# Narrow one-hots of an edge-counting step built by one comparison of two broadcast operands, with packed register words

## The chip, the core and the metric

The kernel runs on one core of a Trainium2 chip. The time is the device time of one execution in microseconds. The engines are named as in the profile: PE (TensorE matmul), PEld (its weight loads), DVE (VectorE), ACT (ScalarE), POOL (GpSimd) and SP (SyncE). A queue item is marked with q, as in DVEq: that is work of the engine's own sequencer (register arithmetic, loads of a register from memory, branches).

## The reference

A graph network on 3125 nodes and 103125 edges, sorted by destination, followed by an edge-conditioned attention layer.

```python
def _L0_gnn_ref(x, edge_index, W1, b1, W2, b2, W3, b3):
    ...
    deg = jax.ops.segment_sum(jnp.ones_like(col, dtype=x.dtype), col, num_segments=N)
    deg_inv_sqrt = jnp.where(deg > 0, jax.lax.rsqrt(jnp.maximum(deg, 1e-12)), 0.0)
    norm = deg_inv_sqrt[row] * deg_inv_sqrt[col]
    def gcn_layer(h, W, b):
        h = h @ W
        msg = norm[:, None] * h[row]
        agg = jax.ops.segment_sum(msg, col, num_segments=N)
        return agg + b
    h = jax.nn.relu(gcn_layer(x, W1, b1))
    h = jax.nn.relu(gcn_layer(h, W2, b2))
    return gcn_layer(h, W3, b3)
...
x = _layernorm(x + _L0_gnn_ref(...), axis=-1)
x = _layernorm(x + _L1_gnn_ref(x, edge_attr_16, ..., src, dst), axis=-1)
```

The first network's three gathers are computed as dense products with a matrix of counts: how many edges lead from each source to each destination. Building that matrix is the step that is changed.

## The kernel before

The counts are an SBUF table of 128 partitions by 25 blocks of destinations. They are filled window by window: a window is 20 destination nodes (WIN), there are 158 windows (NWIN), and a loop of 79 turns does two of them a turn, v = 0 and v = 1. The edges are sorted by destination, 128 to a tile, so a window needs few tiles of edges: six are always done (BASE), and a window that has more does the others one by one in an inner loop, the tail. For each tile DVE builds two one-hot matrices and PE multiplies them, adding the six or more products of a window in one PSUM bank:

- the wide one-hot, `hot_key`, 128 x 500, says for each edge which of 25 source blocks and 20 destinations it has (line 1130);
- the narrow one-hot, `hot_low`, 128 x 128, says which of 128 sources within the block (line 1132);
- PE loads the narrow one as weights and streams the wide one through (line 658). The two windows of a turn go to two banks, named `bank` and `pair` in the rows.

ACT copies each finished bank into the table (line 869). Between its copies ACT also does other work for the ordering of the nodes: 26 passes that count edges below a node (line 852), and 25 rankings (line 923), one in front of every second turn from turn 19 on.

The six tiles go in three groups of two (GROUP). DVE signals s_hot behind a group; PE signals s_hot_free behind its two matmuls. `hot` has four slots, so that two groups are in flight, and a fifth for tails:

```python
for a in range(BASE // GROUP):
    at = v * (BASE // GROUP) + a
    dve.wait_ge(s_hot_free, w * (2 * BASE // GROUP) + at + 1)
    for k in range(GROUP):
        hot_row = one_hot(at % 2 * GROUP + k, v, slice(a * GROUP + k, a * GROUP + k + 1))
    hot_row.then_inc(s_hot, 1)
    if a == 1:
        dve.wait_ge(s_hot, w * (2 * BASE // GROUP) + at)
        near(i * 2 + v + 1, 1 - v).then_inc(s_near, 1)
n = dve.value_load(win_count[0:1, bass.ds(i * 2 + v, 1)], min_val=1, max_val=DEPTH)
```

`near` (lines 1121 to 1126) fetches the next window's numbers: it loads a register with the window's first tile from `win_start`, shifts 16 columns of `edge_key` by the window's offset into `near_key`, and copies 16 columns of `edge_low` into `near_low`. The tile count of a window is loaded from `win_count` by DVE (line 1153) and by PE (line 670). PE ends each window with a drain that signals s_full to ACT (line 676). `plane_tables` (lines 1110 to 1118) fills `win_start` and `win_count` with six short instructions on one partition, once ahead of each of three layers.

When all windows are done, DVE waits for ACT's last copy, and the three gathers and the sorting of edges into units of eight follow; then the long loop of the attention layer, which is 1700 us of the span. None of their code is changed, except that the loops of nodes to themselves are added with another identity matrix (line 1176).

## Time and profile before

| | us |
|---|---|
| median of 3 runs | 2688.94 (2686.95 to 2690.07) |
| profiled execution | 2685.97 |
| its span, first to last instruction | 2684.2 |
| counting stage, about 42 to 664 us of the span | 622 |
| DVE busy in the counting stage | 496.35 |
| PE busy in the counting stage | 457.97 |

The span is divided into stages by what the lines do: preparation to 42 us, counting to 664 us, the gathers and the sorting of edges into units to about 930 us, the attention loop to about 2640 us, and the end. The difference of 1.8 us between the execution and its span lies around the program. The duration of an instruction in a row includes some tens of nanoseconds in which the next one already runs, so the cost of one in a dense sequence is the distance of two starts, not the duration.

### The profile page before, as it was taken

How to read it: one execution, taken by the hardware profiler on the slowest of the kernel's cores; microseconds unless marked ns; L12 is line 12 of the kernel's file. 1: busy time of each engine (PE TensorE's matmuls, PEld its weight loads, DVE VectorE, ACT ScalarE, POOL GpSimd, SP SyncE). 2: the span in 40 equal slices, each digit the busy share in tenths (PEclk: the TensorE clock that was granted, in tenths of full speed). 3: DMA queues.
4: the chain of work that ended last, by engine and by line, in shares of the span. 5: the costliest groups of instructions: out<-in, count | busy, mean ns of one | idle time of the engine just before them, and what ended most of it. 6: DMA issues, size and time to landing. Idle time of an engine off the chain costs nothing.

```text
span 2684.2 us, 39375 instructions
## 1 busy us (share of the span) xinstructions
PE 2030.2 (76%) x5872; PEld 714.5 (27%) x5873; DVE 2113.0 (79%) x4340; ACT 1413.4 (53%) x4967; POOL 1288.1 (48%) x1556
## 2 busy tenths in 40 slices
PE   3766777777699648887888888888888788888782
PEld 1111111111333313333333333333333333333330
DVE  5876888887401149999999999999999889999883
ACT  5123333321001047777767777777776666766762
POOL 2100000012455477666666666666666665666653
PEclk9655555555898859999999999999999999999996
DMA  2000000000000011110000000101000000100110
GB/s 32 14 0 26 0 0 0 0 0 1 20 11 11 16 13 11 10 10 10 10 9 10 10 10 9 10 10 10 9 10 10 10 9 10 9 10 10 10 7 9
DMA packets 87256, 26.29 MB, mean 10 GB/s; under 512 B 63117, under 2 KB 84223, under 8 KB 87103
## 3 DMA queue, kind: packets, MB, share of 16 engines
q0 software_dynamic: 37824, 18.62, 6.4%
q1 hardware_dynamic: 49327, 6.96, 1.7%
q10 hardware_dynamic: 80, 0.43, 0.1%
q8 instruction: 10, 0.16, 0.0%
q14 instruction: 15, 0.12, 0.0%
HBM read 23.30 MB, written 2.51 MB: 10 GB/s over the span
## 4 chain that ended last, share of the span: by engine, by line
issue 28%; DVE 26%; PE 17%; DVEq 15%; POOL 5%; POOLq 4%; ACT 3%; DMA 1%; ACTq 0%; PEldq 0%; SPq 0%; PEld 0%
PE pair L801 10%; DVE eo L1392 7%; DVEq L1409 3%; DVE top L1407 3%; ACT eo L988 3%; PE bank L658 3%; DVE hot L1132 3%; DVE hot L1130 3%; PE pair L658 2%; DVE top L1410 2%; DVE eo L1430 2%; DVEq L1417 2%; DVE rden L1445 2%; DVEq L1153 2%; PE pw L788 1%
## 5 line engine op out<-in xcount | busy, mean ns | idle before, releaser
L617 POOL DMA_INDIRECT nbr<-table,rec x960 | 963.7, 1004 | 463.1 <-issue 258.2
L801 PE MATMUL pair<-eo,ident 128*128 128x512 f32 x1856 | 903.0, 632 | 123.0 <-DVE eo L1430 120.1
L988 ACT ACTIVATE eo<-pw,nbr 128x32 f32<-128x32 f32 x3776 | 686.9, 407 | 0.0
L801 PEld LDWEIGHTS pair<-eo,ident 128*128 128x128 f32 x1856 | 364.8, 202 | 603.1 <-issue 586.9
L1392 DVE TENSOR_TENSOR eo<-pw,nbr 128x1024 f32 (+1 forms) x357 | 417.0, 1218 | 43.4 <-PE pw L788 42.9
L1130 DVE TENSOR_SCALAR hot<-iota_key,near_key 128x500 bf16<-128x500 f16 x974 | 341.0, 350 | 119.3 <-issue 55.5
L788 PE MATMUL pw<-wk,termsT 100*128 100x512 bf16 x954 | 288.5, 384 | 128.6 <-issue 64.6
L977 ACT ACTIVATE eo<-eo 128x2048 f32<-128x2048 f32 x117 | 223.5, 1910 | 206.1 <-DVE eo L1421 206.1
L658 PE MATMUL bank<-hot 128*128 128x500 bf16 x488 | 230.3, 603 | 127.2 <-DVE hot L1132 103.5
L1430 DVE TENSOR_TENSOR eo<-eo x232 | 273.5, 1221 | 30.9 <-issue 27.1
L658 PE MATMUL pair<-hot 128*128 128x500 bf16 x486 | 228.5, 602 | 51.6 <-DVE hot L1132 45.4
L1421 DVE TENSOR_TENSOR eo<-eo,bank (+1 forms) x117 | 266.4, 2277 | 0.0
L1132 DVE TENSOR_SCALAR hot<-iota_low,near_low 128x128 bf16<-128x128 bf16 x974 | 246.3, 253 | 0.0
L966 ACT CAST termsT<-pt 100x512 bf16<-100x512 f32 x240 | 139.3, 581 | 100.9 <-PE pt L770 100.9
L544 POOL TENSOR_SCALAR place<-place 128x25 f32<-128x25 f32 x1 | 0.3, 253 | 384.3 <-ACTq L927 384.3
L770 PE MATMUL pt<-identb,terms 128*100 128x128 bf16 x960 | 95.9, 223 | 116.0 <-ACT termsT L966 87.7
L611 POOL DMA_INDIRECT attr<-in_edge_attr_dram,rec x120 | 115.6, 964 | 136.5 <-DMA rec<-unit_recs 98.4
L869 ACT CAST counts<-pair 128x500 f32 x79 | 45.5, 576 | 225.2 <-PEq L676 225.2
L869 ACT CAST counts<-bank 128x500 f32 x79 | 45.5, 576 | 197.8 <-PEq L676 195.5
L788 PEld LDWEIGHTS pw<-wk,termsT 100*128 100x128 bf16 x954 | 68.1, 97 | 286.7 <-issue 286.4
L1407 DVE TENSOR_TENSOR top<-eo 128x1024 f32 (+1 forms) x117 | 142.7, 1220 | 0.0
L770 PEld LDWEIGHTS pt<-identb,terms 128*100 128x100 bf16 x960 | 78.0, 127 | 235.6 <-issue 235.6
(237 smaller groups left out, 1834.7 us busy)
## 6 DMA issues: line engine op xcount, KB each, us to landing
nbr<-table,rec POOLq DMA_INDIRECT x960, 2.4
rec<-unit_recs SPq DMA_DIRECT2D x122, 8.0 KB, 1.7
attr<-in_edge_attr_dram,rec POOLq DMA_INDIRECT x120, 2.5
unit_recs<-place SPq DMA_DIRECT2D x27, 64.0 KB, 1.6
shared<-key_row SPq DMA_DIRECT2D x1, 1600.0 KB, 6.7
counts<-in_dst_dram SPq DMA_DIRECT2D x1, 448.0 KB
counts<-in_src_dram SPq DMA_DIRECT2D x1, 448.0 KB
place<-in_src_dram,at_i POOLq DMA_INDIRECT x26, 2.6
```

The lines of the kernel that those rows point to most:

```text
L617: pool.indirect_dma_start(nbr[:, b, j * FEAT:(j + 1) * FEAT], None, table, bass.IndirectOffsetOnAxis(ap=rec[:, b, j:j + 1], axis=0)).then_ ...
L658: return pe.matmul(bank[v][:, 0:NG * WIN], hot_low[:, k, :], hot_key[:, k, :], start=first, stop=False, skip_group_check=True)
L788: mm = pe.matmul(pw[:, 2 * (k % 2) + j, :], termsT[:, unit, lo:lo + P], wk[:], start=True, stop=True)
L801: mm = pe.matmul(total, ident[:], eo[:, ring, j * 2 * CH:(j + 1) * 2 * CH], start=False, stop=(j == SLOT - 1), skip_group_check=True)
L977: act.activation(here, here, ACT.Exp).then_inc(s_ex, 1)
L988: done = act.activation(eo[:, ring, lo:lo + wide], pw[:, j - 4, c * wide:(c + 1) * wide], ACT.Copy, scale=nbr[:, held, j * FEAT + c:j * FE ...
L1130: dve.tensor_scalar(hot_key[:, slot, :].rearrange("p (a d) -> p a d", a=NG), iota_key[:], near_key[v][:, k], None, ALU.is_equal)
L1132: return dve.tensor_scalar(hot_low[:, slot, :], iota_low[:], near_low[v][:, k], None, ALU.is_equal)
L1392: dve.tensor_tensor(eo[:, bass.ds(ring, 1), k * 4 * CH:(k + 1) * 4 * CH] .rearrange("p r (c f) -> p (r c) f", f=2 * FEAT), pw[:, 2 * (k % ...
L1407: dve.tensor_tensor(wide(top4[:]), attention(ring, 0, 4), attention(ring, 4, 8), ALU.max).then_inc(s_attr_free, 1)
L1421: dve.tensor_tensor(here, here, wide(after).unsqueeze(1).broadcast_to([P, SLOT, FEAT, FEAT]), ALU.subtract).then_inc(s_d, 1)
L1430: dve.tensor_tensor(here, here, attention(ring, 4 * half, 4 * half + 4), ALU.mult).then_inc(s_p, 1)
```

## The change

The narrow one-hots of a window's six tiles are no longer six comparisons with a scalar per partition. One `tensor_tensor` of 128 x 768 compares the numbers 0 to 127, repeated for six tiles, with six columns of `edge_low`, each repeated 128 times. It stands in `near`, behind the shift of `edge_key`, and writes one of two buffers, `lows[v]`: one in `hot`, the other over `x1`, which is not in use yet. `near_low` and its copy go. `near` is called after the third group instead of the second. `hot` holds six slots instead of four, so that three groups can be in flight, and one for tails.

`win_start` and `win_count` become one table of words, two windows to a word. DVE and PE each load one word a turn (DVE after the first group of v = 1, for the turn behind it; PE after the first group of v = 0) and take first tile and count out of it by register arithmetic. `plane_tables` gets four more short instructions. `identh` goes, its use is taken by `identb`. The copies of `edge_key` and `edge_low` are narrower.

```diff
-        near_low = [sb(f"near_low{v}", [P, DEPTH], BF16, conv) for v in range(2)]
+        lows = [hot_low[:, 0:BASE, :], x1[:].rearrange("p t f -> p (t f)").bitcast(BF16)[:, 0:BASE * P].rearrange("p (k n) -> p k n", n=P)]
...
-                                mm = count(at % 2 * GROUP + k, a == 0 and k == 0)
+                                mm = count(a * GROUP + k, lows[v][:, a * GROUP + k, :], a == 0 and k == 0)
                             mm.then_inc(s_hot_free, 1)
-                        n = pe.value_load(win_count[0:1, bass.ds(i * 2 + v, 1)], min_val=1, max_val=DEPTH)
+                            if v == 0 and a == 0:
+                                pe.reg_mov(pe_word, pe.value_load(win_word[0:1, bass.ds(i, 1)], min_val=0,
+                                                                  max_val=(1 << 2 * WORD) - 1))
+                        pe.reg_alu(pe_n, pe_word, v * WORD, ALU.logical_shift_right)
+                        pe.reg_alu(pe_n, pe_n, DEPTH - 1, ALU.bitwise_and)
...
-            dve.sem_inc(s_hot_free, 2)
+            dve.sem_inc(s_hot_free, BASE // GROUP)
...
+                dve.scalar_tensor_tensor(out=win_row_g[:, 0, :], in0=win_row_g[:, 0, :], scalar=float(DEPTH),
+                                         in1=win_row_g[:, 1, :], op0=ALU.mult, op1=ALU.add)
...
-            def near(window, v):
-                t0 = dve.value_load(win_start[0:1, bass.ds(window, 1)], min_val=0, max_val=NB)
-                dve.tensor_scalar(near_key[v][:], edge_key[:, bass.ds(t0, DEPTH)], win_off[:, bass.ds(window, 1)],
-                                  None, ALU.add)
-                return dve.tensor_copy(near_low[v][:], edge_low[:, bass.ds(t0, DEPTH)])
+            def near(window, v, first):
+                to = dve.snap(first, min_val=0, max_val=NB)
+                key = dve.tensor_scalar(near_key[v][:], edge_key[:, bass.ds(to, DEPTH)], win_off[:, bass.ds(window, 1)],
+                                         None, ALU.add)
+                dve.tensor_tensor(lows[v],
+                                  iota_low[:].unsqueeze(1).broadcast_to([P, BASE, P]),
+                                  edge_low[:, bass.ds(to, BASE)].unsqueeze(2).broadcast_to([P, BASE, P]), ALU.is_equal)
+                return key
...
-                                hot_row = one_hot(at % 2 * GROUP + k, v, slice(a * GROUP + k, a * GROUP + k + 1))
+                                hot_row = hot_keys(a * GROUP + k, v, slice(a * GROUP + k, a * GROUP + k + 1))
                             hot_row.then_inc(s_hot, 1)
-                            if a == 1:
+                            if v == 1 and a == 0:
+                                dve.reg_mov(word_next, word_at(i + 1))
+                            if a == 2:
+                                first_of(1 - v, word if v == 0 else word_next)
                                 dve.wait_ge(s_hot, w * (2 * BASE // GROUP) + at)
-                                near(i * 2 + v + 1, 1 - v).then_inc(s_near, 1)
+                                near(i * 2 + v + 1, 1 - v, first).then_inc(s_near, 1)
```

`hot_keys` is the first half of the old `one_hot`. The tail keeps the comparison with one column for its narrow one-hot, now straight from `edge_low`.

On DVE, the last group of window v = 0 and what follows it up to the test for a tail stood like this before (ISA and REGISTER_ALU are the sequencer's own):

```order
L1145 REGISTER_ALU
L1130 TENSOR_SCALAR hot<-iota_key,near_key0 128x500 [waits s_hot_free]
L1132 TENSOR_SCALAR hot<-iota_low,near_low0 128x128
L1130 TENSOR_SCALAR hot<-iota_key,near_key0 128x500
L1132 TENSOR_SCALAR hot<-iota_low,near_low0 128x128
L1153 ISA
L1153 TENSOR_LOAD win_count
L1153 ISA x2
L1154 COMPARE_AND_BRANCH
```

The same place on DVE in the changed kernel, where line 1160 is the wide one-hot:

```order
L1160 TENSOR_SCALAR hot<-iota_key,near_key0 128x500 [waits s_hot_free]
L1160 TENSOR_SCALAR hot<-iota_key,near_key0 128x500
L1150 REGISTER_ALU
L1140 ISA [waits s_hot]
L1141 REGISTER_ALU
L1141 TENSOR_SCALAR near_key1<-edge_key,win_off 128x16
L1143 ISA
L1143 TENSOR_TENSOR x1<-iota_low,edge_low 128x768
L1185 REGISTER_ALU
L1186 REGISTER_ALU
L1187 ISA
L1188 COMPARE_AND_BRANCH
```

The fetch for the next window, with the wide comparison in it, now stands between the last group and the test for a tail; the register load in front of the test is gone.

On PE, the end of window v = 0 before:

```order
L658 MATMUL bank0<-hot 128x500 [waits s_hot]
L658 MATMUL bank0<-hot 128x500
L670 ISA
L670 TENSOR_LOAD win_count
L670 ISA x2
L671 COMPARE_AND_BRANCH
```

And the whole window on PE in the changed kernel:

```order
L660 MATMUL bank0<-hot 128x500 [waits s_hot]
L660 MATMUL bank0<-hot 128x500
L673 ISA
L673 TENSOR_LOAD win_word
L673 ISA x3
L660 MATMUL bank0<-hot 128x500 [waits s_hot]
L660 MATMUL bank0<-hot 128x500
L668 REGISTER_ALU
L660 MATMUL bank0<-hot 128x500 [waits s_hot]
L660 MATMUL bank0<-hot 128x500
L675 REGISTER_ALU
L676 REGISTER_ALU
```

PE's load has moved from behind the last matmul to behind the second one of v = 0, and window v = 1 has none.

## Rows read from the trace of the kernel before

**Rows 1.** Stretches: length, busy us of PE, PEld, DVE, ACT, POOL; then clock.
```profile
188.00:216.00 28.00, 5.72 (x12) 1.03 (x12) 6.89 (x33) 13.05 (x54) 2.74 (x12) 0.50 0.23 63
...
42.00:664.00 622.00, 457.97 (x973) 83.50 (x974) 496.35 (x2265) 182.77 (x271) 54.78 (x68) 0.55 0.03 6
467.00:477.00 10.00, 5.03 (x18) 1.02 (x18) 8.51 (x42) 4.78 (x5) 0.00 (x0) 1.00 0.00 0
```

**Rows 2.** Group by line, 42 to 664 us: busy us, mean ns, idle.
```profile
L1130 DVE TENSOR_SCALAR hot<-iota_key,near_key 128x500 bf16<-128x500 f16 x974 | 341.0, 350 | 119.3 <-issue 55.5 <-PE bank L658 36.3 <-PE pair L658 25.7
```

**Rows 3.** The timeline of DVE: start, duration, work, idle time before it.
```profile
360.89 0.35 DVE L1130 TENSOR_SCALAR hot<-iota_key,near_key 128x500 bf16<-128x500 f16 x1 [0.64 <-issue]
361.16 0.25 DVE L1132 TENSOR_SCALAR hot<-iota_low,near_low 128x128 bf16<-128x128 bf16 x1
361.32 0.35 DVE L1130 TENSOR_SCALAR hot<-iota_key,near_key 128x500 bf16<-128x500 f16 x1
...
362.75 0.23 DVE L1124 TENSOR_SCALAR near_key<-edge_key,win_off 128x16 f32 x1
362.89 0.17 DVE L1126 COPY near_low<-edge_low 128x16 bf16 x1
363.24 0.35 DVE L1130 TENSOR_SCALAR hot<-iota_key,near_key 128x500 bf16<-128x500 f16 x1 [0.18 <-PE bank L658]
...
364.34 0.35 DVE L1130 TENSOR_SCALAR hot<-iota_key,near_key 128x500 bf16<-128x500 f16 x1 [0.16 <-issue]
...
366.69 0.35 DVE L1130 TENSOR_SCALAR hot<-iota_key,near_key 128x500 bf16<-128x500 f16 x1 [0.22 <-PE pair L658]
...
368.27 0.35 DVE L1130 TENSOR_SCALAR hot<-iota_key,near_key 128x500 bf16<-128x500 f16 x1 [0.64 <-issue]
```

**Rows 4.** The timeline of PE in the same pair of windows.
```profile
362.19 1.84 PE L658 MATMUL bank<-hot 128*128 128x500 bf16 x4 [0.86 <-DVE hot L1132]
...
365.64 1.85 PE L658 MATMUL pair<-hot 128*128 128x500 bf16 x4 [0.39 <-DVE hot L1132]
367.69 1.01 PE L658 MATMUL pair<-hot 128*128 128x500 bf16 x2 [0.20 <-DVE hot L1132]
```

**Rows 5.** The timeline of PE where the clock rises, at 388 us.
```profile
384.37 1.84 PE L658 MATMUL bank<-hot 128*128 128x500 bf16 x4 [0.90 <-DVE hot L1132]
386.41 1.71 PE L658 MATMUL bank<-hot 128*128 128x500 bf16 x3 [0.20 <-DVE hot L1132]
388.52 1.02 PE L658 MATMUL pair<-hot 128*128 128x500 bf16 x4 [0.40 <-issue]
```

**Rows 6.** Queue instructions of the count load: duration in ns, least, median, most.
```profile
L1153 DVEq TENSOR_LOAD <-win_count x158: 299/304/317, 44.8 to 662.8; - x158
...
L1153 DVEq ALU_OP  x79: 40/40/40, 48.0 to 662.8; - x79
```

**Rows 7.** DVE groups by form, whole span.
```profile
L1392 DVE TENSOR_TENSOR eo<-pw,nbr 128x1024 f32 x348 | 406.2, 1218 | 23.2 <-PE pw L788 23.1
...
L1410 DVE TENSOR_TENSOR top<-top 128x512 f32<-128x512 f32 x117 | 81.0, 692 | 10.8
...
L1445 DVE RECIPROCAL rden<-pair 128x256 f32 x25 | 43.8, 1751 | 0.0
...
L1176 DVE TENSOR_TENSOR counts<-counts,identh 128x3072 f16<-128x3072 f16 x1 | 1.8, 1758 | 0.3 <-issue 0.3
```

**Rows 8.** The timeline of ACT around the ranking's start.
```profile
187.31 0.58 ACT L869 CAST counts<-pair 128x500 f32 x1 [2.87 <-PEq L676]
...
212.64 2.96 ACT L923 ACTIVATE gp<-shared,place 128x3200 int8<-128x3200 f32 x1 [14.57 <-DMA shared<-key_row]
```

**Rows 9.** The timeline of POOL behind the last rank, and its next work.
```profile
588.53 0.25 POOL L544 TENSOR_SCALAR place<-place 128x25 f32<-128x25 f32 x1 [384.31 <-ACTq L927]
...
621.42 0.95 POOL L549 DMA_INDIRECT place_records<-place  x1 [0.30 <-issue]
675.70 0.46 POOL L552 PARTITION_ALL_REDUCE deg_max<-deg_p  x1 [53.33 <-DVEq L1235]
```

More of the change, by code:

```diff
@@ L656, in count_plane, with count @@
                     for v in range(2):
-                        def count(k, first):
-                            return pe.matmul(bank[v][:, 0:NG * WIN], hot_low[:, k, :], hot_key[:, k, :],
+                        def count(k, low, first):
+                            return pe.matmul(bank[v][:, 0:NG * WIN], low, hot_key[:, k, :],
                                              start=first, stop=False, skip_group_check=True)
@@ L1103, in _ @@
             windows = dve.alloc_register("dve_windows")
+            word, word_next, first, tiles = (dve.alloc_register(f"dve_{v}") for v in ("word", "next", "first", "count"))
             mid = dve.alloc_register("dve_mid")
```

70 lines of the change are left out of this document (47 added, 23 removed).

## The prediction

> **What bounds the kernel now.** I read the table of stretches first. The counting stage takes 622 us, 23% of the span, and nowhere in it is an engine full: DVE is busy 496 us and PE 458 [rows 1]. So the order of events in one turn of the loop has to be read, in the timelines. DVE starts turns at 360.89 and 368.27, 7.38 us apart [rows 3]. 79 turns are 583 us. The rest of the stage is about 22 us in which the banks wait for ACT (below) and some 17 us for 26 tails: the wide one-hot ran 974 times, 158 x 6 and 26 more [rows 2], so a tail costs about 0.65 us.
>
> Within a turn DVE's sequence sets the pace. A wide one-hot holds DVE 0.27 us (360.89 to 361.16), a narrow one 0.16 (361.16 to 361.32): 12 x 0.43 = 5.1 us [rows 3]. The two fetches and four kinds of idle time make up the other 2.3. Two of these are the sequencer: from the first instruction of the last group to the next window 1.10 us pass at the window turn and 1.58 at the loop turn, though the group's own four instructions hold DVE only 0.85; the rows name "issue" as what ended these idle times, 0.16 and 0.64 [rows 3]. In that chain sits a register load of 0.30 us, where a step of register arithmetic takes 0.04 [rows 6]. At 363.24 and 366.69 DVE waits for PE to free a slot, 0.18 and 0.22 us [rows 3].
>
> PE follows closely, at the lower clock: the stage's mean is 0.55 [rows 1], and nearly all of it is spent at 1.2 GHz. Four matmuls take 1.84 us and two 1.01, so one adds 0.415 us [rows 4]. Between windows PE idles 0.39 and 0.86 us [rows 4]. The 0.39 isn't all waiting for DVE: behind a tail, with DVE ahead, it is 0.40 and ended by "issue" [rows 5]. It is PE's own price for the drain and the branch. The 0.86 has the loop's branch in it as well, and I take it whole.
>
> **DVE after the change.** Per window: six wide one-hots, 6 x 0.27 = 1.6 us; the shift of the keys, 0.14 (362.75 to 362.89) [rows 3]; and the one comparison of 128 x 768. That form isn't in the trace. The nearest rows are f32 tensor_tensors, one of which also reads an operand repeated along the innermost dimension (the 128 x 1024 one with nbr): 512 elements take 692 ns and 1024 take 1218 [rows 7], or 1.03 ns an element. For 768 that is 0.955 us, and since an instruction's duration overlaps the next one's by 0.08 (0.35 against 0.27 [rows 3]), it holds DVE 0.87 us. The sum is 2.61 a window, **5.2** a turn. The two copies of near_low, about 0.1 each, are gone.
>
> The other bound is a 2-byte tensor_tensor of 3072 elements in 1758 ns, 0.57 ns an element, where the repeated operand is a whole row [rows 7]. At that rate 768 elements take 0.55 us and hold DVE 0.47: 4.4 a turn. I take the slower rate, since it is the only one shown for a value repeated within a row. The Trainium skill has a rule for each: "VectorE: DVE Perf Modes", section "The perf-mode tier table", gives tensor_tensor on 2-byte data in SBUF two elements a cycle; "Vector Engine (DVE) Microarchitecture Reference", section 5.1, says that one element read 16 times as either source of such an operation ran at one a cycle. No row here shows the second; by it the turn is 5.2, by the first 4.4 before exposed sequencer time.
>
> The sequencer's chain: the load of 0.30 and the arithmetic on it leave the window turn; steps of 0.04 take their place, some 0.3 us for first tile, count and the two addresses. I estimate 1.0 us at the window turn and 1.45 at the loop turn, from the last group's start. DVE then has 2 x 0.27 + 0.14 + 0.87 = 1.55 us to do, so both are **hidden**. At 0.47 for the comparison it has 1.15, and 0.3 shows at the loop turn: 4.7. The one load a turn that DVE keeps stands behind the first group of v = 1, 0.5 us of work queued ahead of it and the rest of the comparison: nothing. The wait for s_hot in front of the fetch asks for the group before; its last instruction ends while the last group's two run. Behind it only the next window's groups are queued. The wait for a slot goes: three groups are in flight, and a slot is freed a whole window ahead.
>
> **PE after the change.** At 1.2 GHz, with DVE ahead, six matmuls in a row take 1.84 + 2 x 0.415 = 2.67 us. A turn is 2 x 2.67 + 0.39 + 0.86 = **6.6 us**, more than DVE's 5.2. At 2.4 GHz a matmul adds 0.21, six take about 1.02 + 2 x 0.21 = 1.44 [rows 5], and a turn needs 4.1: DVE bounds. PE's load now stands behind two matmuls, which cover it at 1.2 GHz and all but about 0.3 at 2.4, where PE has 1 us to spare. So everything hangs on the clock. What the rows show: the clock rose at 388 us right behind seven matmuls with one short gap, two windows joined by a tail [rows 5]; other rises in the stage look alike. It lasted from 3 to 10 us, as at 467 to 477, where PE was busy half the time at full clock [rows 1]. After the change PE at 1.2 GHz runs six matmuls without the gap of 0.20 in every window, which is closer to what went before the rises than today's four and two; so the half clock ends itself soon. At full clock PE is busier than in those ten microseconds, since the turn is 5.2 and not 7. I take a fifth of the turns at half clock: 0.8 x 5.2 + 0.2 x 6.6 = **5.5 us a turn**.
>
> **The rest.** Turns: 79 x (7.38 - 5.5) = 148.5 us gained. ACT's block of passes and the wait for the key row behind it, from 187.3 to the end of the first ranking at 215.6, doesn't shrink [rows 8]; PE can work one turn into it, now a shorter one: 2 lost. Tails are kept at 0.65, since their two instructions are the same and stand behind the comparison. plane_tables has four more instructions of 0.2 to 0.3 us in a dependent chain, in three layers: 3 to 4 lost, part of it beside the sorting on POOL. The first comparison has nothing in front: 0.7 lost. Narrower copies and identh: under 0.3 gained. Net 148.5 - 2 - 3.5 - 0.7 = **144 us**. What would be late next? ACT ranks 3.15 us at a time in front of two turns; a finished bank is needed again one window later than it is filled, at 2.6 us a window still in time. The chain from the last rank on POOL runs from 588.5 to 622.4, and its successor waits 53 us for DVE [rows 9]; ten turns remain behind the last rank, which shorten by 19, so about 30 us of slack stay. Behind the stage everything starts from its end and moves with it. On the profiled execution's own 2685.97 this gives 2542; from the median of the three runs, 2688.94, it gives **2545**. One execution or the other: the gain is the same.
>
> **Rivals.**
> - The clock stays at 1.2 GHz throughout. PE bounds, a turn is 6.6: 79 x 0.78 = 62 less 6 = 56 gained, 2633. For it: PE still idles 0.39 and 0.86 between windows, and six matmuls are not seven. Against: the rises behind a run that is only one matmul longer. The opposite end, never at half clock, is 79 x 2.18 = 172 less 6: 2523, and lies in the forecast's own range.
> - The comparison runs at the other rate, 0.57 ns an element. With 4.7 at full clock and a fifth at 6.6 the turn is 5.1: 180 less 6, 2515. (The Trainium skill's tier table, named above, would have it so.) For it: the operands have 2 bytes each. Against: the repeated value.
> - Another price in between: a comparison at half the f32 rate holds DVE 1.67 us, the turn is 6.8 at either clock, 2645.
> - Slower than before: the comparison costs so much that DVE's turn exceeds 7.38. That is the case from (7.38 - 2 x 1.74) / 2 = 1.95 us for it on, 2.5 ns an element. The only rows with such a rate are reciprocals, 256 elements in 1751 ns [rows 7]. At 3 ns an element it holds DVE 2.3 us, the turn is 8.1, and the time 79 x 0.7 + 6 = 61 more: 2750. Nothing else in the change has a price of this size.
> - The stage shortens and the time doesn't, since another chain sets the end: the slack of 30 us on POOL speaks against it. Its time would be 2689.
>
> **How the numbers follow.** Forecast 0.64, own range 2520 to 2580 (the clock's share from none to nearly half of the turns); 0.57 ns an element 0.10; half clock throughout 0.16; a price in between 0.05; slower 0.03; no gain 0.02. The range for 8 in 10 is 2505 to 2610: it has the forecast, the case of 0.57 ns and mixtures of the clock up to about four fifths at half. Under 0.2%, 5 us, a measurement of this kernel can't tell from no change; faster by more 0.95, within it 0.02, slower 0.03.
>
> **What would show it.** The comparison's row: about 955 ns and 158 or 159 of them, 550 for the rival. DVE starts 5.2 us apart per turn where PE's clock is full, with no "issue" idle time at the window turn. At half clock 6.6, and there DVE waits for PE. The clock of the stage: about 0.9 by time. The stage about 475 us long, the stages behind it of equal length. I am wrong if the clock stays low, or if the register words cost the sequencer more than the loads did, which would show as "issue" in front of the wide one-hots.

## The result, and the profile after

The changed kernel takes 2529.47 us (median of 4 runs, 2524.33 to 2531.16), where the kernel before took 2688.01 beside it (2686.95 to 2690.07): a ratio of 0.9406 [0.939, 0.9422], 158.5 us faster. The prediction was 2545, range 2505 to 2610. The profiled execution took 2531.16, with a span of 2529.4 us, against 2684.2 before. That is a difference of 154.8 and not 158.5, since this execution was the slowest of its four and the profiled one before was faster than its median.

The table of stretches for the counting stage, now 464 us long (columns as in [rows 1]):

```profile
44.00:508.00 464.00, 294.10 (x974) 72.65 (x974) 427.99 (x1317) 181.29 (x269) 58.30 (x68) 0.88 0.03 8
```

Against the middle line of [rows 1] the stage has shrunk from 622 us to 464. PE is busy 294 us instead of 458 for the same 974 matmuls, since the mean clock rose from 0.55 to 0.88. DVE has 1317 instructions where it had 2265, and is busy 428 of 464 us: now it is nearly full. DVE's groups by form, 42 to 510 us (count | busy us, mean ns of one | idle before them and what ended it):

```profile
L1160 DVE TENSOR_SCALAR hot<-iota_key,near_key 128x500 bf16<-128x500 f16 x974 | 276.2, 349 | 36.0 <-PE bank L660 26.9 <-issue 6.3 <-PE pair L660 2.0
L1143 DVE TENSOR_TENSOR hot<-iota_low,edge_low 128x768 bf16<-128x768 bf16 x80 | 76.1, 951 | 0.0
L1143 DVE TENSOR_TENSOR x<-iota_low,edge_low 128x768 bf16<-128x768 bf16 x79 | 75.1, 950 | 0.0
L1141 DVE TENSOR_SCALAR near_key<-edge_key,win_off 128x16 f32 x159 | 38.1, 240 | 1.1 <-issue 1.1
```

The wide one-hot, the first line, answers to [rows 2]. It had 119.3 us of idle time in front of it and has 36.0; the part ended by "issue" fell from 55.5 to 6.3. Of the 26.9 us put down to PE, 22.2 are one wait, that of ACT's block of passes. The comparison takes 951 ns, 159 times.

The timeline of DVE for one turn at full clock (start, duration, work), which answers to [rows 3]:

```profile
307.06 1.64 DVE L1160 TENSOR_SCALAR hot<-iota_key,near_key 128x500 bf16<-128x500 f16 x6
308.63 0.23 DVE L1141 TENSOR_SCALAR near_key<-edge_key,win_off 128x16 f32 x1
308.76 0.95 DVE L1143 TENSOR_TENSOR x<-iota_low,edge_low 128x768 bf16<-128x768 bf16 x1
309.63 1.63 DVE L1160 TENSOR_SCALAR hot<-iota_key,near_key 128x500 bf16<-128x500 f16 x6
311.18 0.23 DVE L1141 TENSOR_SCALAR near_key<-edge_key,win_off 128x16 f32 x1
311.32 0.95 DVE L1143 TENSOR_TENSOR hot<-iota_low,edge_low 128x768 bf16<-128x768 bf16 x1
312.22 1.65 DVE L1160 TENSOR_SCALAR hot<-iota_key,near_key 128x500 bf16<-128x500 f16 x6
```

From 307.06 to 312.22 it is 5.16 us, and not one row has idle time in front of it. The comparison holds DVE 0.87 us (308.76 to 309.63). PE's timeline, first at full clock and then through a stretch at half clock, answers to [rows 4] and [rows 5]:

```profile
308.56 1.02 PE L660 MATMUL bank<-hot 128*128 128x500 bf16 x4 [0.23 <-issue]
310.29 1.63 PE L660 MATMUL pair<-hot,x 128*128 128x500 bf16 x6 [0.71 <-DVE hot L1160]
...
319.03 2.71 PE L660 MATMUL bank<-hot 128*128 128x500 bf16 x6 [0.91 <-DVE hot L1160]
322.13 2.68 PE L660 MATMUL pair<-hot,x 128*128 128x500 bf16 x6 [0.39 <-issue]
325.72 3.12 PE L660 MATMUL bank<-hot 128*128 128x500 bf16 x7 [0.91 <-DVE hot L1160]
329.24 1.44 PE L660 MATMUL pair<-hot,x 128*128 128x500 bf16 x6 [0.40 <-DVE hot L1160]
```

At half clock a turn of PE is 6.69 us (319.03 to 325.72), six matmuls take 2.68 to 2.71, and the gaps are 0.39 and 0.91. The 0.39 is ended by "issue": it is PE's own. The clock rises at 329.24, behind seven matmuls in a row.

Everything behind the stage has moved and is otherwise as it was. POOL's next work, the line that ends [rows 9], stood at 675.70 with a wait of 53.33 us:

```profile
519.08 0.46 POOL L552 PARTITION_ALL_REDUCE deg_max<-deg_p  x1 [32.81 <-DVEq L1274]
```

It came 156.6 us earlier, with 32.81 us of slack left. The span is shorter by 154.8.

### The profile page after: what moved, and what is told of

Its sections match the earlier page's. It is cut to its first block, busy times and chain, and to the rows that moved or that the text cites. A ratio compares the mean times of both kernels' runs of the same rounds, so it can differ in the third digit from the quotient of the medians.

```text
span 2529.4 us, 38506 instructions
## 1 busy us (share of the span) xinstructions
PE 1866.2 (74%) x5872; PEld 703.7 (28%) x5873; DVE 2047.6 (81%) x3403; ACT 1413.1 (56%) x4967; POOL 1292.2 (51%) x1556
## 4 chain that ended last, share of the span: by engine, by line
issue 28%; DVE 26%; DVEq 16%; PE 15%; POOLq 5%; POOL 4%; ACT 4%; DMA 1%; PEldq 0%; ACTq 0%; PEld 0%; SPq 0%
PE pair L808 11%; DVE eo L1431 7%; DVE hot L1160 4%; ACT eo L995 3%; DVEq L1448 3%; DVE top L1446 3%; DVE eo L1469 2%; DVE top L1449 2%; DVEq L1456 2%; DVE rden L1484 2%; PE pw L795 2%; DVEq L1431 1%; POOLq L566 1%; DVE top L1451 1%; DVEq L1514 1%
## 5 line engine op out<-in xcount | busy, mean ns | idle before, releaser
L1160 DVE TENSOR_SCALAR hot<-iota_key,near_key 128x500 bf16<-128x500 f16 x974 | 276.2, 349 | 36.0 <-PE bank L660 26.9
L660 PE MATMUL bank<-hot 128*128 128x500 bf16 x488 | 149.8, 423 | 134.7 <-DVE hot L1160 91.1
L660 PE MATMUL pair<-hot,x 128*128 128x500 bf16 x474 | 139.7, 418 | 44.1 <-DVE hot L1160 40.9
L804 PE MATMUL pair<-acc,ident 128*128 128x512 f32 x232 | 128.1, 634 | 1.6
L978 ACT ACTIVATE fade<-mdiff 128x256 f32<-128x256 f32 x116 | 48.3, 417 | 141.2 <-DVE mdiff L1457 141.2
```

What stands on the lines that cost most here:

```text
L660: return pe.matmul(bank[v][:, 0:NG * WIN], low, hot_key[:, k, :], start=first, stop=False, skip_group_check=True)
L1160: return dve.tensor_scalar(hot_key[:, slot, :].rearrange("p (a d) -> p a d", a=NG), iota_key[:], near_key[v][:, k], None, ALU.is_equal)
```

## The experiments

**How to read the turns.** The length of a turn is given below as a median over the stage: the distance between the starts of every second near_key, apart for turns that lie wholly at full and wholly at half granted clock. Turns with a tail are left out. I worked these out from the same starts that the timelines show; each timeline here shows one or two of them. The changed kernel's stretches at half clock are short, and in them DVE, with three slots to fill, turns round faster than PE does. The experiments e1 to e4 ran on one chip, where the kernel before took 2688.41 us. The other eight ran on two chips on which the kernel before took 2962.52 and 2963.65 us; there the ratios and the turns are what compares, and the last section says why.

| kernel | ratio to before | turn at full clock, us | turn at half clock, us |
|---|---|---|---|
| before | 1 | 7.03 (one turn) | 7.38 |
| after | 0.9406 [0.939, 0.9422] | 5.16 | 5.6 to 6.5 (PE's own: 6.69) |
| e1: six narrow ones for the wide | 0.975 [0.9734, 0.9766] | 6.37 | 6.37 |
| e2: two groups in flight | 0.9714 [0.9697, 0.973] | 5.75 | 6.84 |
| e3: word loaded and unpacked at each use | 1.0205 [1.0188, 1.0223] | none | 8.07 |
| e4: after, PE kept busy | 0.9383 [0.9367, 0.9398] | 5.16 | none |
| e6: rows for values | 0.948 [0.9457, 0.9503] | 5.07 | |
| e7: pairs for values | 0.9523 [0.9501, 0.9545] | 5.39 | |
| e8: e7, PE kept busy | 0.9534 [0.9518, 0.9551] | 5.38 | |
| e9: before, PE kept busy | 0.9934 [0.9913, 0.9955] | 7.02 | |
| e10: e2, PE kept busy | 0.9624 [0.9597, 0.9652] | 5.75 | |
| e11: comparison, words loaded and unpacked at each use | 1.0204 [1.0169, 1.0239] | none | 8.17 |
| e12: words alone | 0.9928 [0.9901, 0.9955] | 5.73 to 6.01 | 7.38 |
| e13: after again, other chip | 0.9486 [0.9449, 0.9523] | 5.16 | |

### Taking one part out of the changed kernel

**The comparison (e1).**

```
-                dve.tensor_tensor(lows[v],
-                                  iota_low[:].unsqueeze(1).broadcast_to([P, BASE, P]),
-                                  edge_low[:, bass.ds(to, BASE)].unsqueeze(2).broadcast_to([P, BASE, P]), ALU.is_equal)
+                dve.tensor_copy(near_low[v][:], edge_low[:, bass.ds(to, DEPTH)])
+                dve.drain()
+                for k in range(BASE):
+                    dve.tensor_scalar(lows[v][:, k, :], iota_low[:], near_low[v][:, k:k + 1], None, ALU.is_equal)
```

> The changed kernel, with only the wide comparison undone: in the same place of the fetch a copy of 16 columns and six narrow comparisons of 128x128 write the same buffer; register words, three groups in flight and the late fetch stay. Theory (the comparison itself brings little, the rest of the change brings most): six narrow ones hold DVE 6 x 0.16 = 0.96 us, the copy and its drain about 0.25, against 0.87 for the wide one, so +0.33 us a window, a turn of 5.8 us at full clock, and 2565 to 2575. Rival (the comparison is what the change gains from): undoing it gives back most of the 158 us, 2630 or more.

Measured: 2621.77 us (before 2688.41), 92 us over the changed kernel. Neither theory had it. The timeline of DVE, one turn:

```profile
300.47 1.07 DVE L1147 TENSOR_SCALAR x<-iota_low,near_low 128x128 bf16<-128x128 bf16 x6
301.45 0.60 DVE L1162 TENSOR_SCALAR hot<-iota_key,near_key 128x500 bf16<-128x500 f16 x2
302.21 1.13 DVE L1162 TENSOR_SCALAR hot<-iota_key,near_key 128x500 bf16<-128x500 f16 x4 [0.15 <-issue]
...
305.65 1.65 DVE L1162 TENSOR_SCALAR hot<-iota_key,near_key 128x500 bf16<-128x500 f16 x6 [0.52 <-issue]
```

The six narrow one-hots hold DVE 0.98 us (300.47 to 301.45), 0.11 more than the comparison. With the 0.24 of the copy ahead of them that is 0.7 us a turn; the measured 6.37 is 1.2 over 5.16 (times 79: 95 us, the whole loss). The other 0.5 stands in two places, as idle time ended by "issue": 0.15 behind the one load of a turn, between the first and the second group of v = 1 (the 302.21 row), and 0.19 at the loop turn, or 0.52 behind a tail (the 305.65 row). From start to start, without the usual overlap, these are 0.23 and 0.29 us. Here DVE's sequencer has six instructions to pass on where it had one, and it starts on them only when the copy is finished, because of the drain. Which of the two matters more this kernel doesn't tell, since it changed both.

**The third slot (e2).**

```
-            dve.sem_inc(s_hot_free, BASE // GROUP)
+            dve.sem_inc(s_hot_free, 2)
```

> The changed kernel with two groups in flight instead of three (the first credit of s_hot_free is 2, nothing else). Theory: at full clock the third group of a window has to wait about 0.2 us for PE to finish the first, as before the change, so the turn is 5.5 to 5.6 us instead of 5.16 and the time 2550 to 2560. Rival: with the fetch at the window's end PE has caught up anyway and the third slot is worth nothing, 2525 to 2532.

Measured: 2611.16 us, 82 us over the changed kernel, about three times the 21 to 31 that I had expected. DVE at full clock (the first row) and at half clock:

```profile
270.94 0.61 DVE L1160 TENSOR_SCALAR hot<-iota_key,near_key 128x500 bf16<-128x500 f16 x2 [0.17 <-PE bank L660]
...
301.67 1.12 DVE L1160 TENSOR_SCALAR hot<-iota_key,near_key 128x500 bf16<-128x500 f16 x4
303.39 0.61 DVE L1160 TENSOR_SCALAR hot<-iota_key,near_key 128x500 bf16<-128x500 f16 x2 [0.59 <-PE bank L660]
...
306.64 0.61 DVE L1160 TENSOR_SCALAR hot<-iota_key,near_key 128x500 bf16<-128x500 f16 x2 [0.59 <-PE pair L660]
```

At half clock the third group of each window waits 0.59 us for PE. At full clock that wait is 0.17 us, about the 0.2 that I had expected, but it breaks a dense sequence and puts two starts 0.26 us further apart. Twice a turn this makes most of the difference between 5.75 and 5.16, which happens to be 0.59 too, and is 47 us over 79 turns. But a second thing comes with it: a matmul of the stage takes some 495 ns on average, where the changed kernel has 420 and one at full clock 384 (e4); more turns ran at half clock. e10 separates the two. It adds one unused 500-column matmul per window on PE, behind the signal that a bank is full, in a bank that nobody reads in this stage.

> The changed kernel with two groups in flight where it has three, and one unused 500-column matmul per window to keep TensorE busy. With two in flight alone the time rose by 82 us; the turn was 5.75 us at full clock and 6.84 at half clock, and more turns ran at half clock. Theory: the slot waits cost 0.59 us a turn (79 times 0.59 is 47 us) and the rest is the clock that they bring down. With the clock held up the turn is 5.75 throughout, 47 us over the 2522 of the unused matmul alone, about 2570. Rival: the slot waits by themselves cost the 82 us, and the time stays at 2600 or more.

Measured: a ratio of 0.9624 [0.9597, 0.9652] on a chip where the changed kernel has 0.9486 (e13): 0.0138 x 2963.65 = 41 us over it, and with the 7 us that the same matmul gives by itself (e4, below) 48 us over its own reference. By the intervals of the two ratios this can be 14 us more or less, so that the theory's 47 is met more closely than the runs can show. Its stage shows the clock, here from 44 to 508 us of e2 and then of e10:

```profile
44.00:508.00 464.00, 306.04 (x825) 56.79 (x825) 372.60 (x1114) 164.11 (x243) 31.60 (x41) 0.73 0.03 7
```

```profile
44.00:508.00 464.00, 310.27 (x988) 66.33 (x988) 384.52 (x1151) 170.63 (x250) 32.14 (x41) 0.92 0.03 7
```

So of the 82 us some 48 are waits for a slot. The rest goes with the clock: its mean is 0.73 with two slots, 0.88 with three, and 0.92 with two and more work for PE. Slots and clock are one effect with an echo.

**The loads (e3).** The word is loaded from SBUF ahead of each fetch and each tail test on DVE, and ahead of each test on PE.

```
-                            if v == 1 and a == 0:
-                                dve.reg_mov(word_next, word_at(i + 1))
                             if a == 2:
-                                first_of(1 - v, word if v == 0 else word_next)
                                 ...
+                                dve.reg_mov(word_next, word_at(i + v))
+                                first_of(1 - v, word_next)
                                 near(i * 2 + v + 1, 1 - v, first).then_inc(s_near, 1)
+                        dve.reg_mov(word, word_at(i))
```

> The changed kernel with the register loads back in their old places: DVE loads the word before each fetch and before each test for a tail, PE before each test, four loads a turn on DVE instead of one. Theory: each load and its arithmetic are 0.6 to 0.7 us of the sequencer's chain; in front of the fetch DVE has only 0.5 us of work queued, so 0.4 us shows there, and 0.1 and 0.6 show at the window and loop turns: a turn of 6.7 us at full clock, 2630 to 2650. Rival: the sequencer runs ahead far enough behind the wide comparison to hide the loads, 2530 to 2545.

Measured: 2744.11 us, slower than the kernel before by 2%, a hundred over what I had expected; the turn is 8.07 where I had 6.7. DVE, two windows:

```profile
352.66 0.23 DVE L1140 TENSOR_SCALAR near_key<-edge_key,win_off 128x16 f32 x1 [0.62 <-issue]
352.80 0.95 DVE L1142 TENSOR_TENSOR hot<-iota_low,edge_low 128x768 bf16<-128x768 bf16 x1
354.66 1.65 DVE L1159 TENSOR_SCALAR hot<-iota_key,near_key 128x500 bf16<-128x500 f16 x6 [0.91 <-PE pair L660]
356.98 0.23 DVE L1140 TENSOR_SCALAR near_key<-edge_key,win_off 128x16 f32 x1 [0.67 <-issue]
357.12 0.95 DVE L1142 TENSOR_TENSOR x<-iota_low,edge_low 128x768 bf16<-128x768 bf16 x1
358.46 1.65 DVE L1159 TENSOR_SCALAR hot<-iota_key,near_key 128x500 bf16<-128x500 f16 x6 [0.38 <-PE bank L660]
```

Every near_key has 0.62 to 0.67 us of "issue" in front of it, and every next window 0.38 to 0.91. The six wide one-hots run without a gap, so three slots are in use and idle time appears only where a load stands. The fetch has the two instructions of the window's last group ahead of it, 0.5 us of queued work to hide a load under. The profile puts the 0.91 down to PE. PE's matmuls ended 0.9 us before (351.06 + 2.68 = 353.74), so that isn't what was last. The trace has the sequencer's own instructions too, and they fill the time: the load for the tail test starts at 352.81, its arithmetic, the test and the loop's branch follow one another until 354.61, and the one-hot starts at 354.66. The change moved the fetch to a place where it can only stand because the word is already in a register.

### One part of the change alone, on the kernel before

**The comparison without the rest (e11).** The expectation below says that the words aren't packed; in the kernel that ran they are, but each use loads its word anew and unpacks it by two or three steps of arithmetic, which the kernel before doesn't have. Loads stand where they stood before, two groups are in flight, and the fetch is behind the second group. The edit is against the changed kernel:

```
-            dve.sem_inc(s_hot_free, BASE // GROUP)
+            dve.sem_inc(s_hot_free, 2)
...
+                            if a == 1:
+                                dve.reg_mov(word_next, word_at(i + v))
+                                first_of(1 - v, word_next)
+                                near(i * 2 + v + 1, 1 - v, first).then_inc(s_near, 1)
+                        dve.reg_mov(word, word_at(i))
```

> The kernel before with the one wide comparison and nothing else of the change: two groups in flight, the words neither packed nor loaded ahead. Theory: VectorE's work in a turn falls from 5.6 to about 5.1 us and its sequencer has six instructions fewer, but the waits behind the register loads (1.45 us of sequencer work ahead of the end of a turn) and for the slot stay; the turn is 6.2 to 6.6 us where it was 7.4, and the time 2590 to 2630. Rival: in the old order the comparison gives almost nothing, because the loads behind it set the turn, and the time is 2670 or more.

Measured: a ratio of 1.0204 [1.0169, 1.0239]. In this form, with its loads and their unpacking in the old places, the comparison of the change's name leaves the kernel some 60 us slower than before. My theory had 60 to 100 faster. DVE in one turn:

```profile
301.63 0.23 DVE L1140 TENSOR_SCALAR near_key<-edge_key,win_off 128x16 f32 x1 [0.68 <-issue]
301.77 0.95 DVE L1142 TENSOR_TENSOR x<-iota_low,edge_low 128x768 bf16<-128x768 bf16 x1
302.64 0.60 DVE L1159 TENSOR_SCALAR hot<-iota_key,near_key 128x500 bf16<-128x500 f16 x2
303.52 0.61 DVE L1159 TENSOR_SCALAR hot<-iota_key,near_key 128x500 bf16<-128x500 f16 x2 [0.28 <-issue]
304.35 0.61 DVE L1159 TENSOR_SCALAR hot<-iota_key,near_key 128x500 bf16<-128x500 f16 x2 [0.22 <-PE bank L660]
305.47 0.23 DVE L1140 TENSOR_SCALAR near_key<-edge_key,win_off 128x16 f32 x1 [0.51 <-issue]
...
308.00 1.13 DVE L1159 TENSOR_SCALAR hot<-iota_key,near_key 128x500 bf16<-128x500 f16 x4 [0.92 <-issue]
309.79 0.23 DVE L1140 TENSOR_SCALAR near_key<-edge_key,win_off 128x16 f32 x1 [0.66 <-issue]
```

From near_key to near_key of the next pair it is 8.16 us (301.63 to 309.79), of which 0.28 + 0.22 + 0.51 + 0.92 + 0.66 = 2.6 are idle. In [rows 3] the idle times of a turn add up to 1.20. What happened: a group used to consist of four instructions that hold DVE 0.85 us, and now of two, 0.54; the narrow half of its work is gone from there and lies in one block behind near_key. The load ahead of the fetch had been hidden under a group of 0.85 and isn't under one of 0.54. That is one half, 0.31 us, of the idle time that each fetch has gained. The other half is the unpacking, which isn't the comparison's doing. In this row line 1180 takes the first tile out of the word (duration in ns, least, median, most), a step that the kernel before doesn't have:

```profile
L1180 DVEq FUSED_REGOPS  x158: 4/176/518, 46.2 to 755.4; - x158
```

By the sequencer's records, it is 1.05 us from the start of a load to the near_key that needs it, and was 0.76 before. To the next window's first one-hot it is 1.34 at the window turn and 1.86 at the loop turn, and was 1.00 and 1.49 (medians over turns without a tail). With two fetches a turn that is some 1.3 us more, and each of the four chains ends in idle time. The engine's work is some 0.5 us a turn less, the idle time some 1.4 more. Without the unpacking the turn of 8.17 would be about 7.0, by an estimate from these figures, and so shorter than the 7.38 of before. The comparison with the plain loads of the kernel before wasn't run, so whether it alone gains or loses stays open. PE idles along, and its matmuls take 608 to 614 ns on average: the whole stage is at half clock. (The clock column can't be used for it: from 72 to 200 us it reads 1.00, where the matmuls take 614 ns.)

**The words alone (e12).**

```
+                            if v == 1 and a == 0:
+                                dve.reg_mov(word_next, word_at(i + 1))
...
-                        n = dve.value_load(win_count[0:1, bass.ds(i * 2 + v, 1)], min_val=1, max_val=DEPTH)
+                        dve.reg_alu(tiles, word, v * WORD, ALU.logical_shift_right)
```

> The kernel before with the packed words alone: its narrow comparisons, its two groups in flight. Theory: each chain of register work on the queues of VectorE and TensorE loses 0.3 to 0.4 us of which a part was hidden, the engine work stays at 5.6 us, the turn is 6.9 to 7.0 us instead of 7.4, and the time 2650 to 2660. Rival: the words carry most of the gain, and the time is 2600 or less.

Measured: a ratio of 0.9928 [0.9901, 0.9955], 21 us of gain (13 to 29) where I had 29 to 39. The turn, expected at 6.9 to 7.0 us, is two things: 7.38 at half clock, like before, and 5.73 to 6.01 at full. Rows of DVE, the first at half clock, the others one turn apart at full:

```profile
361.64 0.35 DVE L1159 TENSOR_SCALAR hot<-iota_key,near_key 128x500 bf16<-128x500 f16 x1 [0.75 <-PE bank L661]
...
374.59 0.22 DVE L1153 TENSOR_SCALAR near_key<-edge_key,win_off 128x16 f32 x1
...
380.50 0.23 DVE L1153 TENSOR_SCALAR near_key<-edge_key,win_off 128x16 f32 x1
```

At full clock DVE turns round in 5.91 us here (374.59 to 380.50), with its work of 5.6 almost without a gap: the sequencer's share of the old turn, 1.2 us, is gone. At half clock a wait of 0.75 us for a slot stands ahead of a window's last group, where [rows 3] have 0.18 and 0.22: what the sequencer gives back, PE takes. The words' gain is paid out at full clock only, and there the stage seldom was: its matmuls take some 550 ns on average, against 384 at full clock.

### PE kept busy: what the clock is worth

```
+                        pe.matmul(pt[:, 0:NG * WIN], wk[:, 0:P], wk[:, 0:NG * WIN], start=True, stop=True,
+                                  skip_group_check=True)
```

**In the changed kernel (e4).**

> The changed kernel with one more matmul of 500 columns a window on PE, behind the signal of the full bank, into a PSUM bank that nobody reads: work that is of no use. Theory: PE's idle time behind a window is what lets the granted clock fall; the extra matmul fits into the 0.7 to 1.0 us in which PE waits for DVE at full clock, the clock stays at 2.4 GHz nearly all of the stage, every turn takes 5.16 us, and the time falls by some 15 to 20 us to 2510 to 2515. Rival: the clock falls as before, and the extra matmuls only lengthen the half-clock turns from 6.7 to 7.5 us: 2532 to 2540.

Measured: 2522.53 us (2521.95 to 2524.45), 7 us better than the changed kernel, and the fastest version of all. I had expected 15 to 20. The slowest run of this kernel and the fastest of the changed one are only 0.1 us apart, but the traces agree with the 7: the last fetch of the stage starts at 499.4 us, where the changed kernel's starts at 507.0. The stage:

```profile
44.00:508.00 464.00, 329.27 (x1132) 79.27 (x1132) 430.03 (x1327) 183.93 (x272) 57.51 (x68) 0.97 0.04 8
```

Outside ACT's block every turn is at full clock and takes 5.16 us, or 5.93 with a tail. Half clock thus costs the changed kernel 7 us, although a quarter of its stage is spent there (the mean clock is 0.88). Some 27 us of that quarter are ACT's block, in which e4 is at half clock as well. Outside it, from 44 to 158 and from 184 to 499 us, the mean is 0.91, so about 77 us are at half clock. A short stretch of it eats first the 1 us a turn that PE has to spare.

**In the kernel before (e9).**

> The kernel before the change, with the unused matmul of 500 columns a window on PE. It prices the clock in the old kernel alone. Theory: the clock stays at 2.4 GHz, the turn falls from 7.38 to 7.03 us, the value of its one turn at full clock, 79 x 0.35 = 28 us less: 2660. So the clock is a small part of the change's 158 us. Rival: at full clock the waits for a slot go and more with them, 2640 or less; or the extra matmul delays PE and the time is 2688 or more.

Measured: a ratio of 0.9934 [0.9913, 0.9955], 13 to 26 us of gain where 28 were expected. A matmul takes 433 to 455 ns on average, so most of the stage is at full clock, and there the old turn is 7.02 us: the loads set it. So the clock rose because of the change, and was no source of the gain in its own right. The gain needs it all the same. PE's turn at half clock is 6.69, and had it set every turn, 79 x (7.38 - 6.69) = 55 us would have been the most to gain, by this estimate, much as the prediction's rival of half clock throughout has it; the other hundred can be had at full clock only. No run here kept the changed kernel at half clock.

### A faster comparison

**Rows in place of values (e6).** The second operand is a repeated row, so the comparison costs what the cheaper rate of my rival would have it cost. The narrow one-hots are all ones here and the counts are wrong.

```
-                                  edge_low[:, bass.ds(to, BASE)].unsqueeze(2).broadcast_to([P, BASE, P]), ALU.is_equal)
+                                  iota_low[:].unsqueeze(1).broadcast_to([P, BASE, P]), ALU.is_equal)
```

> The changed kernel with the second operand of the wide comparison replaced by the same repeated row of 128 numbers as the first, so the narrow one-hots are all ones and the counts are wrong: it only asks what the repeated single value costs. Theory (a value repeated along the innermost dimension keeps the comparison at one element a cycle, a repeated row doesn't): the comparison takes 550 ns instead of 950, the turn at full clock falls from 5.16 to 4.7 us (the sequencer's loop turn shows), 2490 to 2500. Rival (one element a cycle is the price of two broadcast operands of any kind): 950 ns and 2529.

The comparison takes 551 ns; the turn is 5.07 us, where I had expected 4.7, here and for the prediction's rival, and the changed kernel has 5.16. The ratio of 0.948 [0.9457, 0.9503] can't be told from 0.9486 for the changed kernel on a like chip. DVE:

```profile
L1143 DVE TENSOR_TENSOR hot<-iota_low 128x768 bf16<-128x768 bf16 x80 | 44.1, 551 | 0.0
```

```profile
310.80 0.55 DVE L1143 TENSOR_TENSOR hot<-iota_low 128x768 bf16<-128x768 bf16 x1
311.70 1.64 DVE L1160 TENSOR_SCALAR hot<-iota_key,near_key 128x500 bf16<-128x500 f16 x6 [0.36 <-PE pair L660]
313.26 0.23 DVE L1141 TENSOR_SCALAR near_key<-edge_key,win_off 128x16 f32 x1
313.40 0.55 DVE L1143 TENSOR_TENSOR x<-iota_low 128x768 bf16<-128x768 bf16 x1
313.87 0.61 DVE L1160 TENSOR_SCALAR hot<-iota_key,near_key 128x500 bf16<-128x500 f16 x2
314.68 1.13 DVE L1160 TENSOR_SCALAR hot<-iota_key,near_key 128x500 bf16<-128x500 f16 x4 [0.21 <-issue]
```

The 0.4 us that each comparison gives come back as 0.36 behind the loop's branch and 0.21 behind the one load that is left. The rows put the 0.36 down to PE, but the slot that is needed there was free a microsecond before: it is the first two matmuls of the window before that free it, and in PE's timeline they start at 309.92. Twice 0.40 less 0.36 and 0.21 is 0.23; 0.09 were measured, some of the rest being gaps too short for the timeline to show. The sequencer is the next limit, and it lies only 0.1 us a turn under DVE's work.

**Pairs (e7, e8).** The same rate with the right result: a small copy writes each value twice, and the comparison's innermost dimension is then a pair of neighbours read at step 1. e8 adds the unused matmul.

```
-                                  edge_low[:, bass.ds(to, BASE)].unsqueeze(2).broadcast_to([P, BASE, P]), ALU.is_equal)
...
+                                  near_two[v][:].unsqueeze(2).broadcast_to([P, BASE, P // 2, 2]), ALU.is_equal)
...
+                dve.tensor_copy(near_two[v][:], edge_low[:, bass.ds(to, BASE)].unsqueeze(2).broadcast_to([P, BASE, 2]))
```

> A version that may beat the changed kernel. A copy of 6 columns to 6 pairs (each value twice) is made one group ahead of the wide comparison, which then reads pairs, innermost step 1, repeated 64 times. Theory: the comparison runs at two elements a cycle, 550 ns, the copy holds DVE 0.1 us, and the turn at full clock is 4.8 to 4.9 us with the sequencer's chain behind the shorter comparison showing: 2495 to 2510. Rival (the sequencer's chain or PE's drain bounds the turn once the comparison is short, or a row of two doesn't count as a row): 2525 or more.

> The version with pairs and the unused matmul a window on PE. Theory: the clock stays at 2.4 GHz, every turn is the full-clock turn of the version with pairs, 7 us less than that version, 2488 to 2503. Rival: PE, whose turn is 4.1 us plus 0.4 for the extra matmuls and some load time, becomes the bound and eats the gain: equal to the version with pairs or some us more.

Measured: e7 0.9523 [0.9501, 0.9545], e8 0.9534 [0.9518, 0.9551]. Neither is faster than the changed kernel on a like chip (0.9486, e13). By the ratios they are 11 and 14 us worse, with intervals that overlap. In both the rival came, and not the theory. DVE's groups in e7:

```profile
L1144 DVE TENSOR_TENSOR hot<-iota_low,near_two 128x768 bf16<-128x768 bf16 x79 | 43.5, 551 | 0.0
...
L1152 DVE COPY near_two<-edge_low 128x12 bf16 x158 | 26.8, 170 | 49.3 <-issue 49.3
```

The comparison is fast, 551 ns, but the copy has 49 us of "issue" in front of it. It needs the next window's first tile one group earlier. The idle time stands in front of every second copy, 0.45 to 0.55 us, and these are the ones whose word is loaded just ahead, with one group of 0.54 us to hide the load. The turn is 5.39 us instead of 5.16. A saving on the engine was paid for on the sequencer.

### The changed kernel on the other chips

> The changed kernel unaltered, as the reference for the chip on which the three kernels beside it run. Where the kernel before takes about 2688 us it should take about 2529 again (a ratio of 0.941). On a chip like the one of the pairs experiments, where the kernel before takes about 2960, a fixed gain of 158 us in the counting stage would make the ratio about 0.947, between nothing and 0.2% away from the kernels with pairs (0.952 and 0.953).

Measured: 2811.19 us against 2963.65, a ratio of 0.9486 [0.9449, 0.9523]: 152 us of gain, and the turn is 5.16 us again.

## Why the prediction was right

**Step by step.** The comparison's duration, 0.955 us, was read off f32 rows; 951 ns were measured, and it holds DVE 0.87 as said. The choice of those rows was better than its reason: the row with a repeated value is f32 as well, and can't tell whether the type or the repeated value sets its rate. Only e6 and e7 show that it is the value, at 2 bytes an element. The Trainium skill, "Vector Engine (DVE) Microarchitecture Reference", section 5.1, has one element read 16 times by such an operation at one a cycle; this case agrees for one read 128 times, 951 ns against 551 with a row or with pairs. DVE's turn: 5.2 forecast, 5.16 measured. PE's at half clock: 6.6 and 6.69, though DVE's turns that lie wholly there took 5.6 to 6.5. The gap of 0.39 at the window turn was called PE's own price, and "issue" ends it now with DVE ahead. The load on PE shows 0.23 at full clock (0.3 forecast), hidden by the 0.7 to 0.9 that PE has to spare. The slack on POOL was to shrink to about 30 us and did to 32.8. The stage was to last about 475 us, at a clock near 0.9: 464, at 0.88. No "issue" stands at the window turn.

**The term that was mis-sized** is the clock. I took a fifth of the turns at half clock, 0.2 x 1.4 us x 79 = 22 us over the case of none. e4 measures that term: 7 us. The 15 us between 22 and 7 are about the whole distance from 2545 to 2529.5. The share was nearly right: a fifth of the turns is 24% of the time outside ACT's block, and 18% was measured. The price of one such turn was wrong. At 5.6 to 6.5 us a turn the 77 us are some 13 turns, so one cost about 0.5 us and not 1.4 (an estimate). What I had left out: a turn at half clock costs DVE only what exceeds PE's slack and the slots' depth. Most of the clock's rises did come behind six or seven matmuls in a row, as told, but the one at 233 us came behind runs of two, four and four.

The case of none was put at 2523, and e4, which makes it, takes 2522.53. That close a hit is luck, since small errors offset each other. A tail was taken at 0.65 us and costs 0.77 (5.93 against 5.16), 3 us over 26 tails. The sum as written, 148.5 - 2 - 3.5 - 0.7, is 142.3; its 144 comes from a turn of 5.48 instead of the rounded 5.5. The rival with a price in between, 6.8 us a turn, comes to about 2650 by the same terms, not 2645. And the two rates per element leave out a fixed part of each instruction, about 0.17 us by the two f32 rows: 768 x 0.57 ns alone would be 0.44 us, and the 0.55 given for it, and measured, has that part in it.

**The rivals.** Half clock throughout (2633) didn't come about. The rate of 0.57 ns an element was wrong for this operand; and the time given for it, 2515, was too good as well. e6 had that rate and a turn of 5.07 instead of 4.7. I had allowed 0.3 us for the sequencer in one place of the turn; it shows in two, 0.36 and 0.21, and with gaps too short for the timeline nearly all of the gain is eaten. Break-even against before, set at a comparison of 1.95 us, wasn't tried by size; e3 and e11 show another way to be slower, which no rival of mine had: the comparison at its right price, with loads and their unpacking at each use. The prediction's own sign of being wrong names it, register words that cost the sequencer more than the loads did.

**What the sum hid.** I priced the parts as one turn before and one after, and that was right because all of them were there. I would have been wrong on each alone, and was in the expectations of e1, e2, e3 and e11:

- without the comparison the changed kernel is 92 us slower, without the third slot 82, with the words loaded and unpacked at each use 215; together 389, for a change that gives 158;
- on the kernel before, the words give 21. The comparison without the rest comes out 60 slower, but with the unpacking in it (e11). The comparison with plain loads and the third slot alone weren't tried.

At full clock the words alone and words with the comparison, both with two slots, have nearly the same turn, 5.73 to 6.01 (e12) and 5.75 (e2, e10). Only with the third slot does the comparison's smaller work count, 5.16. Where half clock lasts, PE's own 6.69 is the floor; two slots miss it by 0.16 us (e2) to 0.7 (before and e12), and three let DVE run ahead of it for a short stretch. Each part takes away the bound that stands when the others are in place.

**What stays open.** Whether in e1 the drain or the number of instructions costs more; what the comparison alone would do with the plain loads of the kernel before; and what the changed kernel would take at half clock throughout.

## What to carry to other kernels

When many short instructions become one long one, ask what had been hidden under the short ones: a sequencer's register load needs work queued ahead of it, and here the merging was worth 92 us with the loads out of the way, while with loads at each use, and their unpacking, the kernel was 60 us slower than before. When a load is made to carry more, count the arithmetic behind it at every place that uses it: it was 1.3 us a turn in e11. Price a change as a whole turn on each engine, work and sequencer chain, at both clocks; the slowest of these is the turn, and its parts don't add. A low clock costs only what exceeds the engine's slack, so measure it by keeping the engine busy before paying for it in a sum.

## What the hardware showed beside

**Operands repeated on DVE.** A two-operand comparison of 128 x 768 2-byte elements takes 951 ns when one operand is a single value read 128 times, and 551 ns when that operand is a row, or a pair of equal neighbours, repeated. A copy that makes the pairs is 170 ns for 12 elements a partition.

**Two chips with pauses.** The same kernel took 2529 us on one chip and 2811 on another (e13), in all its runs, as the kernel before took 2688 and 2963. The turn is 5.16 us on both. In the stage of e13 DVE's timeline has pauses of 1 to 7 us, ended by "issue", in two patches; three of the ten:

```profile
69.66 2.08 DVE L1160 TENSOR_SCALAR hot<-iota_key,near_key 128x500 bf16<-128x500 f16 x6 [4.04 <-issue]
...
83.76 0.70 DVE L1160 TENSOR_SCALAR hot<-iota_key,near_key 128x500 bf16<-128x500 f16 x2 [6.74 <-issue]
...
502.41 0.68 DVE L1160 TENSOR_SCALAR hot<-iota_key,near_key 128x500 bf16<-128x500 f16 x2 [4.03 <-issue]
```

The ten add up to 36.1 us, and the last fetch of the stage starts 37 us later than on the first chip (544.2 against 507.0). ACT has such pauses in the same patches, among them 7.04 us ahead of 74.06. What stops the engines there the traces don't show. It is why only ratios and turns of those chips stand beside the first.
